# Reordering a fused cross-attention and feed-forward kernel: attention outputs two slots behind and between the score halves, one block of projections, a later second layer

## The reference, cut to what matters

```python
lat = layer_norm(_layernorm(x)); ctx = layer_norm(context)
q = heads(lat @ Wq); k, v = split(ctx @ Wkv); k = apply_rope(k, cos, sin)
attn = softmax(clip(q @ k.T * 64**-0.5, -11, 11))        # 16 heads, 256 x 512
x = x + (attn @ v) @ Wo + bo
# second layer, per token, on the layer norm xl of x:
h = rmsnorm(xl); q = h @ Wq + bq                          # 16 heads of 8
kv = ((h @ Wdown + bdown) @ Wup + bup).reshape(b, t, 16, 16)
k, v = split(kv)                                          # 8 + 8 per head
out = softmax(q @ k.T / sqrt(8)) @ v                      # 16 x 16 per token
xl = xl + out @ Wo + bo
h2 = rmsnorm(xl); gate = softmax(h2 @ Wg + bg)
x = x + xl + sum_e gate_e * (h2 @ We[e])
```

## Time and profile before

| | |
|---|---|
| median of 3 runs | 353.12 us |
| time of the profiled execution | 353.63 us |
| its span | 351.8 us |
| mean granted TensorE clock over the span | 0.96 |
| TensorE busy | 312.7 us, 89% |
| VectorE busy | 252.5 us, 72% |
| GpSimd busy | 207.1 us, 59% |
| ScalarE busy | 155.4 us, 44% |

### The profile page before, as it was taken

One profiled execution on the slowest core, in us unless ns is written; L12 is line 12 of the kernel. 1 busy time (PEld: TensorE's weight loads), 2 busy tenths in 40 slices (PEclk: granted clock), 3 DMA queues, 4 the chain that ended last, 5 costly groups with the idle time before them and its releaser, 6 DMA issues.

```text
span 351.8 us, 6777 instructions
## 1 busy us (share of the span) xinstructions
PE 312.7 (89%) x2584; PEld 212.5 (60%) x2584; DVE 252.5 (72%) x470; ACT 155.4 (44%) x287; POOL 207.1 (59%) x206
## 2 busy tenths in 40 slices
PE   6769999999999999959999999949999999987762
PEld 6547666666676655636686655626676655857441
DVE  3955734434876479997848689896538497799977
ACT  3535564555543555532437374733335466020330
POOL 4526664533665486673836576982545688755661
PEclk9986999999999999987999999987999999999899
DMA  7843112111111111110101110111101100000001
GB/s 225 233 123 72 43 45 62 47 31 41 37 32 31 31 33 30 33 30 17 46 1 34 28 39 23 32 30 32 32 2 46 30 2 2 16 2 0 0 0 30
DMA packets 16318, 14.23 MB, mean 40 GB/s; under 512 B 4832, under 2 KB 11808, under 8 KB 16288
## 3 DMA queue, kind: packets, MB, share of 16 engines
q1 hardware_dynamic: 15232, 13.69, 14.7%
q10 hardware_dynamic: 1056, 0.13, 0.2%
HBM read 4.89 MB, written 0.52 MB: 15 GB/s over the span
## 4 chain that ended last, share of the span: by engine, by line
PE 62%; DVE 26%; ACT 5%; issue 3%; DMA 2%; POOL 1%; SPq 0%; ACTq 0%; DVEq 0%; POOLq 0%
PE pv L589 16%; PE sc L575 15%; PE sums L605 6%; PE pj_k L513 6%; DVE o L1308 5%; ACT e L803 4%; PE pj_k L515 4%; PE pj_k L514 4%; PE side L676 3%; DVE att L1155 2%; DVE o L1311 2%; DVE ks L993 2%; DVE prod L976 2%; DMA sin_in<-in_L_xattn_sin_dram 2%; PE side L720 1%
## 5 line engine op out<-in xcount | busy, mean ns | idle before, releaser
L1497 POOL TENSOR_SCALAR e<-e 128x1024 f32<-128x1024 f32 x64 | 68.9, 1077 | 78.1 <-ACT e L803 71.6
L803 ACT ACTIVATE e<-sc 128x1024 f32<-128x1024 f32 x64 | 65.7, 1027 | 83.2 <-PE sc L575 83.2
L575 PE MATMUL sc<-qs,ks 64*128 64x256 f32 x768 | 64.5, 302 | 5.7 <-ACT e L803 5.0
L575 PEld LDWEIGHTS sc<-qs,ks 64*128 64x128 f32 x768 | 51.2, 191 | 28.8 <-issue 18.2
L589 PE MATMUL pv<-e,v 128*64 128x256 f32 x512 | 65.8, 401 | 0.0
L1490 POOL TENSOR_TENSOR krot<-kcos,kswap 128x512 f32<-128x512 f32 x32 | 41.3, 1290 | 17.6 <-DMA kswap<-ksin 9.5
L589 PEld LDWEIGHTS pv<-e,v 128*64 128x64 f32 x512 | 35.2, 142 | 24.5 <-issue 9.3
L1057 DVE TENSOR_TENSOR ksin<-pj_k,sinT 128x512 f32<-128x512 f32 x32 | 22.1, 690 | 36.2 <-PE pj_k L515 32.4
L993 DVE TENSOR_TENSOR ks<-krot,ks 128x512 fp32r<-128x512 f32 x32 | 33.1, 1035 | 0.0
L811 ACT ACTIVATE u<-pv 128x256 f32<-128x256 f32 x32 | 12.3, 385 | 43.7 <-PE pv L589 43.7
L605 PE MATMUL sums<-e,sum_rows 128*32 128x256 f32 x512 | 30.9, 382 | 0.0
(11 more groups left out here) (261 smaller groups left out, 559.9 us busy)
## 6 DMA issues: line engine op xcount, KB each, us to landing
kswap<-ksin SPq DMA_DIRECT2D x128, 64.0 KB, 2.0
ctx_in<-in_ctx_dram SPq DMA_DIRECT2D x4, 256.0 KB, 3.1
prod<-in_L_xattn_Wkv_dram SPq DMA_DIRECT2D x2, 512.0 KB, 6.0
x_in<-in_x_dram SPq DMA_DIRECT2D x1, 512.0 KB, 5.8
prod<-in_L_xattn_Wq_dram SPq DMA_DIRECT2D x1, 512.0 KB, 6.6
wo<-in_L_xattn_Wo_dram SPq DMA_DIRECT2D x1, 512.0 KB, 8.3
fwe<-in_L_ffn_We_dram SPq DMA_DIRECT2D x1, 512.0 KB, 4.3
out_dram<-x_in SPq DMA_DIRECT2D x3, 128.0 KB, 1.8
```

The costliest lines, as they stand in the source:

```text
L575: last = nc.tensor.matmul(sc[:, h, c * NT:(c + 1) * NT], ks[rows, j % 3, k_part, chunk], qs[rows, j % 2, q_part, :], start=(k_part + q_par ...
L803: nc.scalar.activation(e[:, j % 3, :, 2 * half:2 * half + 2, :].rearrange("p h c n -> p h (c n)"), sc[:, :, :], ACT.Exp, scale=SCALE).then ...
L1497: nc.gpsimd.tensor_scalar(a, a, EXP_HIGH, EXP_LOW, ALU.min, ALU.max).then_inc(s_clip, 1)
```

## The change

Six things change together.

- **Outputs.** `times_values` runs two slots behind the scores instead of one, and stands between the two score halves. The last two pairs' outputs stand at the end (`outputs_at`). ScalarE's copy moves with it.
- **Projections.** Values, keys and queries stand as one block at the end of a slot, and queries run two slots ahead instead of one. VectorE's key_products and query_lo move to the end of its slot, key_lo to its beginning; ScalarE's query_hi moves behind key_hi; GpSimd's rotate moves behind the first clip.
- **Side steps.** o_T goes from position (8, b) to (10, c), out_proj2 to (11, a), h2_T to (12, c), gate to (13, a), moe0 and moe1 to (14, b) and (14, c), lat_T to (5, b).
- **Own steps.** reciprocals go from the middle to the end of VectorE's slot, reduce_1 behind key_lo, the later steps follow the side steps; both of GpSimd's expert sums stand at (16).
- **Layout.** The columns of keyval2 are put in another order once (`order_columns`, four activations on ScalarE in slot 6), so that the keys of all heads are contiguous and the values of all heads for one coordinate lie side by side. weighted_values then reads its values with step 1 instead of 16.
- keyval2 waits for that reordering in the first batch.

```diff
+QUERIES_AHEAD = 2
+
+OUTPUTS_BEHIND = 2
...
-    (3, "c"): "h_T", (4, "a"): "query_down", (4, "b"): "keyval2", (8, "b"): "o_T", (8, "c"): "out_proj2",
-    (10, "c"): "h2_T", (11, "a"): "gate", (13, "b"): "moe0", (13, "c"): "moe1", (15, "a"): "moe2",
+    (3, "c"): "h_T", (4, "a"): "query_down", (4, "b"): "keyval2", (10, "c"): "o_T", (11, "a"): "out_proj2",
+    (12, "c"): "h2_T", (13, "a"): "gate", (14, "b"): "moe0", (14, "c"): "moe1", (15, "a"): "moe2",
...
-    "reciprocals": [(0, "mid")],
+    "reciprocals": [(0, "end")],
...
-    "reduce_1": [(8, "early")],
-    "root_norm": [(10, "first")],
-    "gate_exps": [(11, None)],
-    "gates": [(11, "late")],
+    "reduce_1": [(8, "mid")],
+    "root_norm": [(11, "end")],
+    "gate_exps": [(13, None)],
+    "gates": [(14, "first")],
...
-    "mean_square": [(9, 1)],
-    "sum_experts_0": [(13, 1)],
-    "sum_experts_1": [(16, -1)],
+    "mean_square": [(11, 1)],
+    "sum_experts_0": [(16, 0)],
+    "sum_experts_1": [(16, 1)],
...
-PREP_STEPS = {(3, "b"): "ctx_T", (6, "a"): "lat_T"}
+PREP_STEPS = {(3, "b"): "ctx_T", (5, "b"): "lat_T"}
...
+def outputs_at(slot):
+
+    if slot == NPAIR:
+        return [], [NPAIR - 1]
+    between = [slot - OUTPUTS_BEHIND] if slot >= OUTPUTS_BEHIND else []
+    return between, [NPAIR - 2] if slot == NPAIR - 1 else []
...
                 elif name == "keyval2":
+                    if b == 0:
+                        pe.wait_ge(s_kv_columns, 4)
...
-                                                fwup[:, :], start=True, stop=True)
+                                                fwkv[:, :], start=True, stop=True)
...
-                if slot + KEYS_AHEAD < NPAIR:
-                    keys(slot + KEYS_AHEAD)
+                between, behind = outputs_at(slot)
                 if 0 <= slot < NPAIR:
                     scores(slot, 0)
+                for j in between:
+                    times_values(j)
                 side_at(slot, "a")
-                if 0 <= slot + 1 < NPAIR:
-                    queries(slot + 1)
+                if 0 <= slot < NPAIR:
+                    scores(slot, 1)
+                if slot < NPAIR:
...
                 if 2 <= slot <= NPAIR and slot % 2 == 0:
                     sums(slot - 1)
-                if 0 <= slot < NPAIR:
-                    scores(slot, 1)
...
                 for n in value_units(slot):
                     values(n)
                 side_at(slot, "b")
-                if 1 <= slot <= NPAIR:
-                    times_values(slot - 1)
+                if slot + KEYS_AHEAD < NPAIR:
+                    keys(slot + KEYS_AHEAD)
+                if 0 <= slot + QUERIES_AHEAD < NPAIR:
+                    queries(slot + QUERIES_AHEAD)
...
                     exps(slot, 0)
+                for j in between:
...
-                if 0 <= slot + 1 < NPAIR:
-                    query_hi(slot + 1)
...
+                for j in behind:
+                    attention_copy(j)
...
+                side_taken(slot, "b")
                 if 0 <= slot + KV_AHEAD < NPAIR:
                     key_hi(slot + KV_AHEAD)
-                side_taken(slot, "b")
-                if 1 <= slot <= NPAIR:
-                    attention_copy(slot - 1)
+                if 0 <= slot + QUERIES_AHEAD < NPAIR:
+                    query_hi(slot + QUERIES_AHEAD)
...
                 gate_exps(slot)
+                if slot == PAIRS - 2:
+                    order_columns()
...
-            v_v = kv2[:, t, :].rearrange("p (g c) -> p c g", g=G)[:, GD:2 * GD, :]
+            v_v = kv2[:, t, D:2 * D].rearrange("p (c g) -> p c g", g=G)
...
-                if slot + KEYS_AHEAD < NPAIR:
-                    key_products(slot + KEYS_AHEAD)
                 if more and p == 4:
                     split_ctxT(b + 1)
+                if more and p == 6:
+                    split_latT(b + 1)
                 second_layer(slot, "first")
+                if 0 <= slot and slot + 1 < NPAIR:
+                    key_lo(slot + 1)
...
+                second_layer(slot, "early")
                 side_taken(slot, "a")
-                second_layer(slot, "early")
-                if 0 <= slot + 1 < NPAIR:
-                    query_lo(slot + 1)
-                if more and p == 6:
-                    split_latT(b + 1)
-                if 0 <= slot + 1 < NPAIR:
-                    key_lo(slot + 1)
                 second_layer(slot, "mid")
                 second_layer(slot, "late")
                 side_taken(slot, "b")
...
+                if slot + KEYS_AHEAD < NPAIR:
+                    key_products(slot + KEYS_AHEAD)
+                if 0 <= slot + QUERIES_AHEAD < NPAIR:
+                    query_lo(slot + QUERIES_AHEAD)
+                if slot == -1:
+                    key_lo(0)
...
-                if 0 <= slot + KV_AHEAD < NPAIR:
-                    rotate(slot + KV_AHEAD)
                 second_layer(slot, -1)
                 if 0 <= slot < NPAIR:
                     clip(slot, 0)
+                if 0 <= slot + KV_AHEAD < NPAIR:
+                    rotate(slot + KV_AHEAD)
```

39 lines of the change are left out of this document (29 added, 10 removed).

## The result

| | before | after |
|---|---|---|
| median, range | 352.91 us, 352.27 to 353.14 (4 runs) | 360.3 us, 358.42 to 366.41 (4 runs) |
| ratio after / before | | 1.0195, 95% interval 1.0129 to 1.026 |
| profiled execution, its span | 353.63, 351.8 us | 366.41, 364.6 us |
| mean granted clock over the span | 0.96 | 0.931 |

The profiled execution of after is a slow one, 366.41 us at a granted clock of 0.931 where the other three show 0.943 to 0.959, and the ratios are taken without such executions. The forecast was 338 us, its range 329 to 347. Against the mean of the other three, 359.7 us, the miss is some 21 us.

The account below looks back on a forecast made before the run. TensorE's own list was taken to bound steady slots, with VectorE setting the pace twice; -6.2 - 7.2 - 3.3 + 2.5 - 1.1 = -15.3 from 353.6 us gave 338.3, 338 as a median, range 329 to 347.

Parts of the forecast that it names:

- Outputs between the halves, -6.2: Between TensorE's score halves: outputs placed there fill the wait for the exponentials, -6.2 us.
- The full holes: TensorE idle between score halves, 0.64 us each in nine slots; eight of them were to close, 5.1 us.
- Small new waits: Extra waits for keys in some slots, values, row sums and key_lo, over three batches, +2.2 us.
- One block, -7.2: TensorE's projections: joining keys, queries and values saves tile-shape changes of 0.2 us, 36 times, -7.2 us.
- Later o_T, -3.3: Second layer: moving o_T later removes TensorE's waits for VectorE, less new waits elsewhere, -3.3 us net.
- The three waits at norm0: TensorE waiting for recS at norm0 in slots 9, 17 and 25: +1.5, +3.9 and +2.0 us.
- the credit, -12.9: TensorE's idle at o_T in slots 16 and 24, 8.5 us, and the slow stretches behind it go, -12.9 us.
- Head, +2.5: Start of the kernel: scores start at about 26.7, +1.6 us, and open holes in slots 0 and 1, +0.9; +2.5.
- Layout, -1.1: VectorE's weighted_values fall from 1.93 to 1.22 us; two in the tail count, less GpSimd's last sums, -1.1 us.
- A: Rival: VectorE's backlog bounds slots 12-17 and 20-25; waits move to norm0 with the slow clock; 346 us, chance 0.20.
- B: Rival: VectorE instructions stretched beside GpSimd shrink, so norm0 waits fall from 7.4 to about 1.5; 331 us, chance 0.12.
- C: Rival: the key path stretches beyond two slots and lengthens every slot; 369 us at an 18 us path, chance 0.04.

Follow-up runs that it names:

- The kernel with the cover: Kernel before with outputs moved between the score halves, plus the next slot's keys moved ahead of side step c on TensorE: 351.15 us, ratio 0.9948.
- the high query first: The changed kernel with query_hi put ahead of key_hi in ScalarE's list: 358.64 us, ratio 1.0173 against the kernel before.

## Why the prediction was wrong, by its own steps

- *Outputs between the halves, -6.2.* The full holes closed as counted. The step that failed is that nothing was charged for the place the outputs left. "Small new waits", +2.2, had to hold it; alone it is 10.9 us of side bank, and the part costs 4.7 us net where 6.2 were to be gained. The kernel with the cover shows it: 7.0 us fewer of these waits, 5.8 us less time.
- *One block, -7.2.* In the undisturbed slots it is there (a slot with no hole, like slot 8, went from 7.01 to 6.82 us; the first two query matmuls start 0.23 us apart where they follow scores, 150.86 to 151.09 in before, and 0.12 where they follow keys, 162.28 to 162.40 in after). Undoing it inside the change moved the time by no more than the noise, so as a whole it brought nothing there. Where its gain was spent is argued, not shown: undone, the exponentials' waits fell by 5.9 us, and the side bank's rose by 5.5.
- *Later o_T, -3.3.* The three waits at norm0 were forecast at 1.5, 3.9 and 2.0 us and came as 1.97, 3.27 and 4.03: right in kind, 1.9 too small together. The 3.9 against 3.27 in slot 17 is partly luck. From keyval2 to that norm TensorE needed 34.2 us, not 31.9, and VectorE 37.3, not 35.8, of which it stood idle 3.4 for GpSimd, a wait that had no term. The slow stretch counted in its credit is in the trace of before: times_values takes 3.68 us behind the wait in slot 16, where the granted clock was 0.50 (158.60 to 162.30), and 1.95 in slot 7, at 1.00. What failed is the credit, -12.9: alone, the part is 3 us slower, since the wait and its slow clock moved to the next steps of VectorE's list, and the expert sums reached the last reciprocals.
- *New waits without a term in after*: exponentials in slots 14 to 30 5.7 us, the side bank 5.5, the low key in slot 12 1.1, sums 1.4. These 13.7 less the 2.2 allowed are over half of the miss. With the high query first, in a faster execution, they are 4.7, 6.0, 1.1 and 1.4.
- *Head, +2.5.* The order was right, the size not: scores start at 28.79 (forecast 26.7) in this profile, in others of the same head 26.9 to 28.5. Slots 0 and 1 take 14.4 us; 13.3 before, with 1.9 of outputs in them, so 3.0 where 0.9 was taken. This term hangs on when the clock rises: here slots 0 and 1 both stand at 0.50, and with the high query first slot 1 is at 1.00 and the two take 11.7.
- *Layout, -1.1.* Its price was right to 0.01 us an instruction. Its worth was entered under o_T's backlog, together with the later steps that were to remove the same wait. Alone it is worth 6.5 us by its ratio: two edits were credited against one wait, and the one that takes work away kept it.
- *Rivals.* A, that the wait moves to norm0 and takes the slow clock along, was the nearest, though the slow clock did not come with every wait (0.75 in slot 25 of after, 1.00 in slot 17); at 346 it lacked the other waits. B, that recS is no longer stretched beside GpSimd, did not come in slot 25, where its two last steps take 1.05 and 1.44 us. C (slower by the key path of every slot) is not what happened: of the slots only slot 12 waits for a low key.
- *The parts and the whole.* By their ratios outputs, later steps and layout alone give +5.0, +3.1 and -6.5 us, +1.6 together, and the change +6.9. The other 5 us lie in the joined block, in the orders that came with it and in what the parts do to each other; no run separates these.

## What to carry to other kernels

Before a block is moved out of an in-order list, ask what it covers where it stands: which shared buffer is emptied meanwhile, and by which engine. The waits that came from VectorE's backlog were shortened by taking work from VectorE (at o_T from 3.75 and 4.71 to 2.66 and 2.77 us); moving the step that waits handed them to the next reader in VectorE's list, until the list's order was mended too (3 us lost without, 1.6 gained with it). Test the parts alone: here the smallest forecast term, 1.1 us, brought 6.5, and the 6.2 of the outputs were a loss of 4.7.

## What the runs showed of the hardware

VectorE's two steps on recS take 0.29 and 0.56 us in the layout's kernel, and 1.32 and 2.43 with GpSimd's weighted values beside them; the reciprocal ahead of them takes 1.76 in both.

The ends say what the size is. The second step ends at 297.63, 0.28 us after GpSimd's second product (297.35), and the first at 295.17, 0.16 after its first (295.01). The division of slot 16 in the kernel before ends at 153.35 and GpSimd's product at 153.20 (VectorE, then GpSimd):

```profile
150.62 2.73 DVE L1311 TENSOR_TENSOR o<-o,aden 128x128 f32<-128x128 f32 x1
```
```profile
150.29 2.91 POOL L976 TENSOR_TENSOR prod<-att,kv 128x1024 f32<-128x1024 f32 x1
```

The same division takes 0.29 us at 157.57, with GpSimd idle. In the 20 traces, 62 of these divisions and 53 of the second steps on recS began while a GpSimd instruction ran that left them no time to end by themselves, and all of them ended 0.14 to 0.15 and 0.27 to 0.29 us after it. So the price of these is not a factor but what is left of the GpSimd instruction. By an estimate, each VectorE instruction's time less the shortest of its kind in all traces, products and weighted values left out, this holding is 4.2 us of VectorE's busy time in slots 12 to 16 of the kernel before and 7.4 in slots 20 to 24. The waits at o_T there, 3.75 and 4.71, came from a list that was full partly for this reason.
